# Expert blocks: token rows loaded in pieces of 32 numbers and turned on VectorE instead of TensorE

## The reference

```python
logits = -dist2 + jnp.einsum('bld,ed->ble', x, rw) + rb
topv, topi = jax.lax.top_k(logits, TOP_K)
w = jax.nn.softmax(topv, axis=-1)
hidden = jax.nn.gelu(jnp.einsum('bld,efd->blef', x, w1) + b1, approximate=False)
exp_out = jnp.einsum('blef,edf->bled', hidden, w2) + b2
sel = jnp.take_along_axis(exp_out, topi[..., None], axis=2)
fused = jnp.sum(w[..., None] * sel, axis=2)
```

## Time and profile before

| | us |
|---|---|
| median of 3 runs | 1123.17 |
| lowest, highest | 1119.8, 1127.43 |
| profiled execution | 1132.63 |
| its span, first to last instruction | 1130.8 |
| mean granted TensorE clock, share of full | 0.982 |
| TensorE busy | 1073.6 (95%) |
| VectorE busy | 828.3 (73%) |
| ScalarE busy | 839.5 (74%) |
| GpSimd busy | 696.9 (62%) |

### The profile page before, as it was taken

One profiled execution on the slowest core, in us unless ns is written; L12 is line 12 of the kernel. 1 busy time (PEld: TensorE's weight loads), 2 busy tenths in 40 slices (PEclk: granted clock), 3 DMA queues, 4 the chain that ended last, 5 costly groups with the idle time before them and its releaser, 6 DMA issues.

```text
span 1130.8 us, 27458 instructions
## 1 busy us (share of the span) xinstructions
PE 1073.6 (95%) x8485; PEld 870.8 (77%) x8486; DVE 828.3 (73%) x2568; ACT 839.5 (74%) x2050; POOL 696.9 (62%) x890
## 2 busy tenths in 40 slices
PE   8999999999999999999999999997998789999993
PEld 4677777777777777777777777775888789999992
DVE  6788888888889888978888888985453234447764
ACT  5788887888888888878778888876664456666661
POOL 4554456765775676577577577657565656666563
PEclk9999999999999999999999999999998999999996
DMA  8776666766766776677576667878324222243552
GB/s 218 221 210 189 190 166 182 227 185 165 231 188 177 216 196 188 177 210 211 156 209 205 166 195 206 253 228 266 124 77 133 70 62 74 74 129 93 151 153 65
DMA packets 138223, 193.27 MB, mean 171 GB/s; under 512 B 19320, under 2 KB 110976, under 8 KB 138096
## 3 DMA queue, kind: packets, MB, share of 16 engines
q1 hardware_dynamic: 128944, 174.84, 54.5%
q0 software_dynamic: 9152, 16.88, 4.4%
HBM read 103.27 MB, written 90.33 MB: 171 GB/s over the span
## 4 chain that ended last, share of the span: by engine, by line
PE 82%; DMA 5%; issue 5%; DVE 3%; another core or an unknown queue 2%; ACT 1%; SPq 1%; POOL 1%; ACTq 0%; DVEq 0%; POOLq 0%
PE bank L1300 15%; PE bank L1428 12%; PE bank L1337 10%; PE bank L1314 9%; PE bank L1326 9%; PE bank L1348 4%; PE bank L1251 4%; PE bank L1253 3%; PE bank L1252 3%; PE bank L1417 3%; PE bank L1415 3%; PE bank L1416 3%; DMA pt_d<-pt_dram 2%; DMA pt_dram<-turned 2%
## 5 line engine op out<-in xcount | busy, mean ns | idle before, releaser
L808 POOL TENSOR_SCALAR shared<-shared,rinv 128x512 f32<-128x512 f32 x512 | 350.1, 695 | 229.6 <-DVE rinv L1038 226.3
L876 ACT ACTIVATE shared<-shared,nmax 128x512 f32<-128x512 f32 x512 | 368.4, 733 | 77.0 <-DVE nmax L1032 60.2
L1032 DVE CUSTOM_DVE_ANT_0 shared<-bank,shared 128x512 f32<-128x512 f32 x512 | 330.3, 683 | 83.4 <-issue 35.4
L843 POOL DMA_INDIRECT y_dram<-yb,home x158 | 174.3, 1103 | 122.8 <-issue 85.3
L1428 PE MATMUL bank<-shared,act_h 128*128 x1264 | 162.1, 283 | 14.5 <-DVE yb L1154 10.1
L1048 DVE STREAM_TRANSPOSE turned<-shared 128x512 f32<-128x512 f32 x256 | 166.3, 689 | 12.5 <-issue 10.1
L365 POOL DMA_INDIRECT xs_dram<-copies,slot x128 | 134.5, 1051 | 62.1 <-issue 51.9
L1428 PEld LDWEIGHTS bank<-shared,act_h 128*128 128x128 f32 x1264 | 151.8, 196 | 23.1 <-issue 23.1
L882 ACT ACTIVATE pt_e<-bank 128x512 f32<-128x512 f32 x256 | 145.2, 596 | 18.0 <-PE bank L1314 17.2
L908 ACT ACTIVATE act_h<-bank,shared 128x256 f32<-128x256 f32 x316 | 125.0, 477 | 30.3 <-PE bank L1417 14.9
L1314 PE MATMUL bank<-idn,shared 128*128 128x128 f32 x1024 | 136.4, 276 | 0.5 <-DVE nmax L1032 0.5
(11 more groups left out here) (154 smaller groups left out, 1877.5 us busy)
## 6 DMA issues: line engine op xcount, KB each, us to landing
pt_dram<-turned SPq DMA_DIRECT2D x512, 128.0 KB
pt_d<-pt_dram SPq DMA_DIRECT2D x128, 512.0 KB
xb<-xs_dram SPq DMA_DIRECT2D x79, 129.0 KB
shared<-in_experts SPq DMA_DIRECT2D x16, 514.0 KB
shared<-y_dram SPq DMA_DIRECT2D x32, 256.0 KB
shared<-roll_dram SPq DMA_DIRECT2D x4, 768.0 KB, 8.3
y_dram<-yb,home POOLq DMA_INDIRECT x158
xs_dram<-pad_sb SPq DMA_DIRECT2D x17, 129.0 KB, 2.2
```

Source lines behind the costliest of these rows:

```text
L808: pool.tensor_scalar(tile, tile, rinv[:, 2 * v + hh:2 * v + hh + 1], 1.0, ALU.mult, ALU.mult)\
L843: pool.indirect_dma_start(y_dram, bass.IndirectOffsetOnAxis(ap=home[:, j, c:c + 1], axis=0), yb[:, j, c, :], None, bounds_check=last_row, ...
L876: act.activation(prob[:, v, hh, :], prob[:, v, hh, :], ACT.Exp, bias=nmax[:, n:n + 1], scale=-1.0, accum_out=rsum[:, n:n + 1]).then_inc(ex ...
L1032: dve.tensor_tensor_reduce(prob[:, v, hh, :], score_bank(v, hh)[:], strips[:, 2 * i + hh, v * P:v * P + S], -1.0, BIG, ALU.add, ALU.min, n ...
```

## The change

- `xb` holds a block in another layout. Partition group g (32 partitions) gets numbers 32g to 32g + 31 of every row: partition 32g + s, piece k is row 32k + s of the block. Four DMAs load it, each with 32 x 8 pieces of 32 numbers (128 bytes). They all count on `ld_xb`.
- The 129th numbers come by a fifth DMA into `home_f`, 256 pieces of 4 bytes, with its own semaphore `ld_home`; `home` is made from `home_f`.
- VectorE turns 32x32 squares of the whole `xb` tile (128x256) in one instruction into a new SBUF tile `xbt`, two buffers. It does so one block ahead: `turn_rows(m + 1)` stands in block m behind `expert_lo(m)` and ahead of the sums; in `drain` it is placed by hand.
- `turned_hi` and `turned_lo` read `xbt` in place of bank 0. `turn` and its waits leave TensorE.

```diff
-        xb = sb("xb", [P, UN, BC, D + 1])
+        xb = sb("xb", [P, UN, BLK // BK, BK])
+        xbt = sb("xbt", [P, 2, BLK])
+        home_f = sb("home_f", [P, UN, BC])
...
-                sp.dma_start(xb[:, j], xs_dram[bass.ds(row, BLK), :].rearrange("(p c) d -> p c d", c=BC)).then_inc(ld_xb[j], 16)
+                here = xs_dram[bass.ds(row, BLK), :]
+                for g in range(D // BK):
+                    sp.dma_start(xb[g * BK:(g + 1) * BK, j], here[:, g * BK:(g + 1) * BK].rearrange("(k s) r -> s k r", s=BK))\
+                        .then_inc(ld_xb[j], 16)
+                sp.dma_start(home_f[:, j, :], here[:, D:D + 1].rearrange("(c p) d -> p (c d)", p=P),
+                             allow_slow_non_contiguous=True).then_inc(ld_home[j], 16)
...
-                act.activation(xbt_hi[:, q % 2, :], ps_xt[:, 0:BLK], ACT.Copy).then_inc(xbhi_rdy, 1)
+                act.activation(xbt_hi[:, q % 2, :], xbt[:, q % 2, :], ACT.Copy).then_inc(xbhi_rdy, 1)
...
+            def turn_rows(m, q):
+
+                j = q % UN
+                dve.wait_ge(ld_xb[j], 16 * (D // BK) * (m // UN + 1) if isinstance(m, int) else (m - j) * (16 * (D // BK) // UN) + 16 * (D // BK))
+                dve.transpose(xbt[:, q % 2, :], xb[:, j].rearrange("p k r -> p (k r)")).then_inc(xbt_rdy, 1)
+
             def turned_lo(m, q):
                 dve.wait_ge(xbhi_rdy, m + 1)
-                dve.tensor_tensor(xbt_lo[:, q % 2, :], ps_xt[:, 0:BLK], xbt_hi[:, q % 2, :].bitcast(F32),
+                dve.tensor_tensor(xbt_lo[:, q % 2, :], xbt[:, q % 2, :], xbt_hi[:, q % 2, :].bitcast(F32),
                                   ALU.subtract).then_inc(xblo_rdy, 1)
...
-                dve.tensor_copy(home[:, j, :], xb[:, j, :, D]).then_inc(home_rdy, 1)
+                dve.tensor_copy(home[:, j, :], home_f[:, j, :]).then_inc(home_rdy, 1)
...
             def block_dve(m, j):
                 turned_lo(m, j)
                 expert_lo(m, j)
+                if not isinstance(m, int) or m + 1 < NBLK:
+                    turn_rows(m + 1, j + 1)
...
             def drain():
+                turn_rows(0, 0)
+                turn_rows(1, 1)
                 turned_lo(0, 0)
                 expert_lo(0, 0)
                 turned_lo(1, 1)
+                turn_rows(2, 2)
                 expert_lo(1, 1)
                 turned_lo(2, 2)
+                turn_rows(3, 3)
                 expert_lo(2, 2)
                 finish(0, 0)
                 turned_lo(3, 3)
+                turn_rows(4, 4)
...
-            def turn(m, q):
-
-                j = q % UN
-                if not isinstance(m, int) or m >= 1:
-                    pe.wait_ge(xblo_rdy, m)
-                pe.wait_ge(ld_xb[j], 16 * (m // UN + 1) if isinstance(m, int) else (m - j) * (16 // UN) + 16)
-                for c in range(BC):
-                    mm = pe.transpose(ps_xt[:, c * P:(c + 1) * P], xb[:, j, c, 0:D], idn[:])
-                mm.then_inc(xbt_rdy, 1)
...
             def block_pe(m, j):
-                turn(m, j)
```

More of the change, by code:

```diff
@@ L236, in layer_kernel @@
         yk = shared[:, NE * EW:NE * EW + YB * TOP * S].rearrange("p (a k c d) -> p a k c d", k=TOP, c=TC, d=D)
-        ps_xt, ps_y, ps_h = banks[0], banks[1], (banks[2:4], banks[4:6])
+        ps_y, ps_h = banks[1], (banks[2:4], banks[4:6])
         def hidden_bank(q, f):
@@ L246, in layer_kernel @@
         ld_xb = [sem(f"ld_xb{j}") for j in range(UN)]
+        ld_home = [sem(f"ld_home{j}") for j in range(UN)]
         xbt_rdy, xbhi_rdy, xblo_rdy, w1hi_rdy, w1lo_rdy = (sem(n) for n in (
@@ L1148, in finish @@
                 w = dve.snap(at[LAG + q], min_val=0, max_val=(NE - 1) * EW)
-                dve.wait_ge(ld_xb[j], 16 * ((m - j) // UN + 1) if isinstance(m, int) else (m - j) * (16 // UN) + 16)
+                dve.wait_ge(ld_home[j], 16 * ((m - j) // UN + 1) if isinstance(m, int) else (m - j) * (16 // UN) + 16)
                 if not isinstance(m, int) or m >= UN:
                     dve.wait_ge(y_sent[j], (m - j) * (BC * 16 // UN))
-                dve.tensor_copy(home[:, j, :], xb[:, j, :, D]).then_inc(home_rdy, 1)
+                dve.tensor_copy(home[:, j, :], home_f[:, j, :]).then_inc(home_rdy, 1)
                 dve.wait_ge(y_mm, m + 1)
@@ L1493, in step @@
                 if exists(one[0]):
-                    if (b, i) == (LAST, NPR - 1):
-                        pe.wait_ge(neg_rdy, NB * CHUNKS)
-                        turn(0, 0)
                     weigh_early(*one)
@@ L1507, in drain @@
                 weights_t(LAST, NPR - 1, 3, 1)
-                turn(1, 1)
                 weigh_late(LAST, NPR - 1)
                 hidden(1, 1)
-                turn(2, 2)
                 second(0, 0)
                 weigh_early(LAST, NPR - 1)
-                turn(3, 3)
                 hidden(2, 2)
```

## The result

The changed kernel takes 1141.41 us (median of 4 runs, 1140.37 to 1145.12), the kernel before beside it 1123.82 (4 runs): ratio 1.0156, 95% interval 1.0126 to 1.0186. That is 17.6 us slower; the forecast was 5 us faster, and the range ended at 1140. The profiled execution of after has 1141.09 us, span 1139.2; that of before had a span of 1130.8, so the two traces show 8.4 of the 17.6 us.

A forecast was written before the change was run, and what follows sets the result against it. It took one block in two as bound by TensorE's instructions, the other by a late report of its result. -7.8 us removed and +2.6 at the start made -5.2, from 1123.2 to 1118 us, range 1103 to 1140.

The forecast's parts named there:

- What is removed (-7.8 us): Transposes leaving TensorE: 0.22 us gained in every two blocks, 0.11 a block, 7.8 us in all.
- the late report: In every other block TensorE's result reaches yb 3.12 us after `second` starts, not 2.19; taken to stay unchanged.
- the first rival's dispatch gain: Rival: every block gains the full 0.22 us on TensorE, -16.5 us, giving 1109 us; chance 0.24 (full gain or more).
- The start (+2.6 us): 15 load issues instead of three between two halves of the last attention exchange delay `pt_d` by 2.6 us.
- the upper bound of 4.6: Largest start delay foreseen, 4.6 us, if small packets also hold `pt_d` up in the DMA engines.
- SyncE's queue in steady state (nothing): Five DMAs a block take 2.4 us of issue, below 3.56 us a block, so they cost nothing.
- these 17 us: SyncE's queue's lead: a load is issued some five blocks before its transpose; pad stores and sums' loads use part.
- the sign that I named as proof of expensive packets: The new VectorE transpose waiting for xb in steady state would prove the small-packet price wrong.
- VectorE (nothing): The added 128x256 transpose takes 0.42 us a block, 33 us in all, inside VectorE's idle time; cost nothing.
- The third rival, VectorE and start: Rival: transpose delays yb in the last 24 blocks (+5), start costs 4.6, gain only 3: +7, 1130 us; chance 0.16.
- DMA engines (nothing): 1360 packets a block at 20.6 ns take 1.75 us over 16 engines; cost nothing below about 36 ns.
- "slower by more": Chance 0.23 of a slowdown beyond about 1%: the DMA-bound rival and part of the VectorE-and-start rival.

The follow-up runs named there:

- a1_after: The changed kernel, unedited, run again on a slow chip: 1148.72 us, 1.0135 of the kernel before.
- e10_before_small: Kernel before plus four small-piece loads a block into a spare tile, turned by VectorE into another; TensorE keeps its transposes; slow chip: 1146.47 us, 1.0116.
- e1_start: Changed kernel with only block 0 loaded ahead of the second half of the last attention exchange; fast chip: 1094.64 us, 1.0003 of before.
- a0_after: The changed kernel, unedited, run again on a fast chip: 1102.05 us, 1.0051 of the kernel before.
- e9_one_fill: Changed kernel with the old single load (true transposition left out) and two idle TensorE transposes in blocks 4 to 78; slow chip: 1135.58 us, 1.0014 of before.
- h2_five_big: Changed kernel with the old load (true transposition left out) cut into five DMAs of 1032-byte pieces; fast chip: 1090.61 us, 0.9948 of before.

## Why the prediction was wrong

**What is removed (-7.8 us): this step failed. On the kind of chip of the result it was nothing, on the other more than forecast.** It took the late report as a thing of a `second` that follows `hidden`, which stays as it is when `turn` goes: 3.12 us kept, and 2.19 kept for the other. The traces show 2.19 and 3.1 us where two transposes stand behind `second`, 2.7 and 3.4 where none do, and then most blocks wait for the report, not every other one. In the trace of the result a block gains 0.06 us, not 0.11; in the pair `a1_after` and `e10_before_small` nothing is gained. The earlier trace rows had it: 3.34 us for a `second` with no `turn` about it. I read it as "still late" beside 3.12 and left the 0.22 of difference unexplained. Where the report is prompt and a block has one load, the first rival's dispatch gain is near: 12.0 us measured by two instructions, 0.22 us a block in the stretch 30 to 58, against its 16.5. The chip of the result was not of that kind, and I had no row to tell me that there are two.

**The start (+2.6 us): right chain, wrong size.** 15 issues take 10.2 us, 0.68 each, not 0.48; `pt_d` comes 5.56 us later, beyond the upper bound of 4.6. The price was that of three large loads; small pieces cost more in the queue (8.83 against 7.48 us for 15). That it was on the path shows in `e1_start`, whose `pt_d` is issued 5.2 us and whose first yb starts 5.8 us before those of `a0_after` (two fast chips).

**SyncE's queue in steady state (nothing): this step failed too, and it is the larger error.** With the start, the loads were to cost 2.6 us; they cost 11 to 13.5 on the slow kind of chip and 19.7 on the fast. I compared 2.4 us of issue with 3.56 us a block and called the rest slack. The slack was in the rows, as a total: 132.4 us of waiting. Four more issues a block, at my own 0.48 us, are 76 x 1.92 = 146 us. The queue was to run out of slack by that sum alone, with the pad stores and the fetches of the sums still to pass in it. In the trace of after the wait is 2.7 us. What was late next was not the row load on that chip but the fetch for the sums (by 5.5 us more than the blocks at its first issue), of which I had said that it "uses part of these 17 us"; VectorE then waits 7.8 us where it waited 0. In `a1_after` it waits only 1.2 us for them, so on the slow kind of chip the traces don't place the whole cost. On the fast chip, where TensorE needs 3.2 us a block, the transpose itself waits for rows, 13.4 us: the sign that I named as proof of expensive packets comes, mainly at least, from the queue that issues them.

**VectorE (nothing): right.** 0.437 us for the transpose (0.42 taken), and 0.9996 with the work added alone, on a fast chip. The third rival, VectorE and start, had the right sign and the start in it, but nothing shows its VectorE part.

**DMA engines (nothing): right in size.** 12.8 ns a packet where I took 20.6, and 36 was the point at which it decides. The Trainium skill, "DMA: Bandwidth & Descriptors", Specifications, wants 512 bytes for line rate. This trace has 0.70 MB in 29.0% of 20 us over 16 engines against 0.79 MB in 16.3% before: the rule agrees, half the rate. As a transfer it costs nothing that these runs show: on the slow chip five large pieces are no faster than the small ones (1.0122 and 1.0135), and the fetches of the sums land no later beside small packets.

**The sum.** On the slow kind of chip the loads cost 10.9 us (`e10_before_small` less `e9_one_fill`) or 13.5 (less the kernel before), and the removal gains nothing; in the traces of the result the start shows 5.6 us of it and the stretch with the sums 4.2. The other 4 to 7 of 17.6 us aren't settled: the two profiled executions differ by 8.4 us where the medians differ by 17.6, and the 2 to 3 us by which blocks 30 to 58 are longer without TensorE's transposes (106.0 against 103.6) show in another chip's traces, not in that pair. The 0.23 for "slower by more" stood on the DMA engines and VectorE alone; the queue of issues was in none of the rivals.

## What to carry to other kernels

A DMA cut in parts is paid in the queue that issues it: multiply the added issues by their spacing over the whole stage, and set the product against the total that this queue waits, then name what stands behind the loads in it. Instructions taken off a bounding engine were worth nearly their length only where that engine waited neither for a report of its own nor for late loads; put idle ones back in their place, and the difference is their worth. A time that differs between chips must be compared with the kernel before on the same chip: 28 to 39 us lie between the kinds, more than any effect here.

## What was not expected of the hardware

- Two kinds of chip: the same program takes 1094 to 1096 us on four of them, 1124 and 1133 on two. On the latter, yb follows `second` by 2.19 or 3.1 us where it is 2.09 on the former, and between 842 and 921, blocks 11 to 26, yb waits seven times for up to 5.4 us (31.4 in all) for something that the profile can't name, and TensorE stops behind it. Blocks 10 to 30 take 95.4 us there, 69.3 on the other kind. The cause wasn't found.
- On that kind, the time from a group of matmuls to its reader goes with what TensorE does right after it: 2.2 us with two transposes behind, mostly 2.7 without. What in them does it wasn't tried.
- 12.8 ns for the mean packet where nearly all have 128 or 4 bytes, on the hardware queue, where the mean packet of the loads of 1032 bytes took 60.
- The 16 pad stores take 11.87 us of SyncE's queue in `a0_after`, 0.74 each (10.03 in `h2_five_big`), a load of 256 pieces of 128 bytes 0.46 (1.84 for four).
